# Reordering the seam between attention and the per-row blocks, and the first feed-forward tiles, of a fused transformer layer on one core

## The reference

```
x = x + attention(x)          # 32 query heads on 8 KV heads, 512 cached + 128 new keys, RMS norm, rotary, softmax
x = x + linear1(x) + low1(x)  # 512x512, and a rank-32 product chosen per row, times 0.5
x = x + linear2(x) + gated(x) # 512x512, 8 experts of rank 16; gates: top 2 of x @ Wr.T + 5*one_hot(language)
x = x + down(silu(gate(x)) * up(x))   # width 1376, each of the three with a rank-16 product chosen per row
```

## Time and profile before

| | us |
|---|---|
| median of 3 runs | 1445.12 |
| range of the 3 runs | 1442.46 to 1446.32 |
| the profiled execution, its own time | 1446.37 |
| span of the profiled execution | 1444.6 |
| PE busy (share of the span) | 1393.5 (96%) |
| DVE busy | 1100.4 (76%) |
| ACT busy | 843.5 (58%) |
| POOL busy | 808.4 (56%) |
| mean granted PE clock, share of full | 0.991 |

### The profile page before, as it was taken

One profiled execution on the slowest core, in us unless ns is written; L12 is line 12 of the kernel. 1 busy time (PEld: TensorE's weight loads), 2 busy tenths in 40 slices (PEclk: granted clock), 3 DMA queues, 4 the chain that ended last, 5 costly groups with the idle time before them and its releaser, 6 DMA issues.

```text
span 1444.6 us, 26952 instructions
## 1 busy us (share of the span) xinstructions
PE 1393.5 (96%) x8004; PEld 1210.6 (84%) x8004; DVE 1100.4 (76%) x2209; ACT 843.5 (58%) x2072; POOL 808.4 (56%) x801
## 2 busy tenths in 40 slices
PE   2899999999999999999999999999999999899999
PEld 1788888888888888888888888888888788688887
DVE  4788888888888888888888888888888566554544
ACT  1566666666666666666666667676676322433332
POOL 5555555555555666666666666666566320454342
PEclk9899999999999999999999999999999999999999
DMA  4433343333333322232322222222323440233441
GB/s 127 138 103 110 114 117 101 101 103 103 103 101 104 95 71 66 65 76 68 70 64 65 65 69 76 66 67 47 116 59 94 114 96 22 91 120 120 121 120 67
DMA packets 192705, 129.87 MB, mean 90 GB/s; under 512 B 119088, under 2 KB 159792, under 8 KB 190256
## 3 DMA queue, kind: packets, MB, share of 16 engines
q1 hardware_dynamic: 192560, 128.15, 32.1%
HBM read 125.24 MB, written 24.64 MB: 104 GB/s over the span
## 4 chain that ended last, share of the span: by engine, by line
PE 81%; SPq 12%; issue 3%; DVE 1%; DMA 1%; POOL 1%; ACT 1%; DVEq 0%
PE banks L311 19%; PE banks L312 19%; PE banks L313 19%; PE banks L1275 10%; PE banks L1252 8%; SPq L357 6%; SPq L341 3%; SPq L365 2%; PE banks L1216 2%; DMA w_raw<-in_w_att 1%; PE banks L1490 1%; PE banks L1504 1%; PE banks L1317 1%; PE banks L1443 1%; SPq L336 1%
## 5 line engine op out<-in xcount | busy, mean ns | idle before, releaser
L695 ACT ACTIVATE prob<-prob,nbias 128x640 f32<-128x640 f32 x256 | 210.4, 822 | 148.6 <-DVE nbias L908 148.6
L883 DVE TENSOR_TENSOR pt_pair<-banks,pt_pair 128x640 fp32r<-128x640 f32 x256 | 211.0, 824 | 108.3 <-ACT pt_pair L691 105.7
L908 DVE CUSTOM_DVE_ANT_0 prob<-banks,mask,q_rs 128x640 f32<-128x640 f32 x256 | 220.3, 879 | 42.8 <-PE banks L313 42.6
L1275 PE MATMUL banks<-w_pair,o_pair 128*128 128x512 f32 x768 | 224.1, 414 | 0.0
L691 ACT ACTIVATE pt_pair<-banks 128x640 fp32r<-128x640 f32 x256 | 179.3, 700 | 44.1 <-PE banks L1252 44.1
L311 PE MATMUL banks<-w_pair,x_pair 128*128 128x256 f32 (+1 forms) x512 | 179.1, 350 | 20.9 <-POOL w_pair L489 20.9
L1252 PE MATMUL banks<-ident,prob 128*128 128x128 f32 x1280 | 185.3, 276 | 3.5 <-DVE pt_pair L883 3.5
L1252 PEld LDWEIGHTS banks<-ident,prob 128*128 128x128 f32 x1280 | 147.4, 140 | 45.2 <-issue 33.2
L312 PE MATMUL banks<-w_pair,x_pair 128*128 128x256 f32 (+1 forms) x512 | 174.0, 340 | 0.0
L313 PE MATMUL banks<-w_pair,x_pair 128*128 128x256 f32 (+1 forms) x512 | 173.3, 339 | 0.0
L311 PE MATMUL banks<-kt_pair,qt_pair 128*128 128x320 f32 x512 | 164.9, 322 | 2.2 <-DVE kt_pair L883 2.2
(11 more groups left out here) (176 smaller groups left out, 3433.4 us busy)
## 6 DMA issues: line engine op xcount, KB each, us to landing
w_raw<-in_w_att SPq DMA_DIRECT2D x64, 320.0 KB, 3.2
w_raw<-in_fw SPq DMA_DIRECT2D x66, 256.0 KB, 3.3
x_raw<-in_xT SPq DMA_DIRECT2D x64, 256.0 KB, 3.2
kt_all<-in_kT SPq DMA_DIRECT2D x128, 128.0 KB, 2.5
kv_raw<-in_kv SPq DMA_DIRECT2D x416, 32.0 KB, 1.6
kt_raw<-kt_all SPq DMA_DIRECT2D x38, 256.0 KB, 3.0
kv_raw<-in_kv SPq DMA_DIRECT2D x608, 16.0 KB, 1.5
fb_all<-in_gu_b SPq DMA_DIRECT2D x32, 176.0 KB
```

The lines of the kernel that those rows point to most:

```text
L695: act.activation(prob[:, h, :], prob[:, h, :], ACT.Exp, bias=nbias[:, h:h + 1], scale=-1.0, accum_out=psum_row[:, h:h + 1]).then_inc(exped, 1)
L883: dve.tensor_tensor(pair[1], src, pair[0].bitcast(F32), ALU.subtract).then_inc(lo_sem, 1)
L908: dve.tensor_tensor_reduce(out=prob[:, h, :].rearrange("p (a n) -> p a n", a=2), in0=score_ps[h % 2][:, :, 0:HALF], in1=mask[:, n % B, :]. ...
L1275: last = pe.matmul(misc_ps, o_pair[:, j, h, :], w_pair[:, k, ds(at + h * HID, HID)], start=i == 0, stop=i == 3 * REP - 1)
```

## The change

Only the order of instructions changes; each engine has as many as before.

1. Row 0's x1 transposes on PE move from step 63 into step 62, behind the output projection's middle eight matmuls and ahead of the third probability transposes; ACT's copy and DVE's split of them move to the end of step 62. The low-rank product `lora1(0)` moves ahead of the last probability transposes of step 62 on PE, and ACT's `low_high(0)` and DVE's `lora1_low(0)` move forward in step 63.
2. In step 63 ACT does the fourth exponential ahead of the second probability copy.
3. `gu_high(0, 0)` moves from the start of stage 6 into stage 5, behind `low_high(6)`. `gu_high(1, 1)` moves from the first feed-forward step into the end of stage 6. On DVE `fb_low(0, 0)` moves to the end of stage 6 and `fb_low(1, 1)` ahead of `end_b(7)`.
4. ACT's `dn_high(0, 0)` and the sigmoid of tile 0 go ahead of the last `x3t_high`; DVE's two multiplications of tile 0 (`gated(0)`) ahead of the last `x3t_low`. Splitting `act_pair` stays in the first feed-forward step.
5. The copy and split of `db_pair` move from just before the feed-forward to behind step 4 of it.

The core of the diff:

```diff
@@ ACT, attention step
                 if n == NT - 2:
+                    x1t_high(0)
                     act.wait_ge(s_b1, 16 * 4)
@@ ACT, final_step
                 pt_high(n - 1, 3)
-                x1t_high(0)
+                low_high(0)
                 v_high(n, par)
                 exponent(n, par, 2)
                 o_high(n - 1)
                 pt_high(n, 0)
-                low_high(0)
                 to_high(ra_pair[:, 0], ra_raw[:], s_small, 16 * 6, ra_hi)
+                exponent(n, par, 3)
                 pt_high(n, 1)
-                exponent(n, par, 3)
@@ ACT, stage
                 low_high(b + 1)
+                if b == B - 3:
+                    gu_high(0, 0)
                 hgt_high(b)
                 x2t_high(b + 1)
                 if b + 2 < B:
                     x1t_high(b + 2)
+                else:
+                    gu_high(1, 1)
@@ ACT, after the stages
+            def ff_step(m, par):
+                if m > 1:
+                    gu_high(m, par)
+                    dn_high(m - 1, 1 - par)
+                    sigmoid(m - 1)
+                act_high(m - 1, 1 - par)
             for b in range(1, B - 1):
-                if b == B - 2:
-                    gu_high(0, 0)
                 stage(b)
...
             hgt_high(B - 1)
+            dn_high(0, 0)
+            sigmoid(0)
             x3t_high(B - 1)
-            act.wait_ge(s_ffs, 16 * 5 * B)
-            act.activation(db_pair[:, 0], d_b[:], ACT.Copy).then_inc(db_hi, 1)
@@ DVE, attention step, behind add_attention(n - 1)
+                if n == NT - 2:
+                    x1t_low(0)
@@ DVE, final_step
                 normalise(n, 1)
-                x1t_low(0)
                 mask_min(n, par, 2)
...
+                lora1_low(0)
                 normalise(n, 2)
                 o_low(n - 1)
                 pt_low(n, 0)
-                lora1_low(0)
@@ DVE, after the stages
+            fb_low(0, 0)
             gate_up_lora(0)
...
-            fb_low(0, 0)
+            fb_low(1, 1)
             end_b(B - 1)
+            gated(0)
             x3t_low(B - 1)
-            low(db_hi, 1, [db_pair[:, k] for k in range(2)], d_b[:], db_lo)
@@ PE, x1_transpose
+                if b == 0:
+                    pe.wait_ge(qt_lo, NT)
@@ PE, attention step
                     project_out(n - 1, 2, 10)
+                if n == NT - 2:
+                    x1_transpose(0)
                 transpose_p(n, 2)
@@ PE, final_step
                 scores(n, 1)
+                lora1(0)
                 transpose_p(n - 1, 3)
-                x1_transpose(0)
                 scores(n, 2)
                 values(n - 1, 1 - par, False)
-                lora1(0)
```

More of the change, by code:

```diff
@@ L704, in w2_high, with to_high, x1t_high @@
                 act.activation(w2_pair[:, 0, c, :], w2_raw[:, c * HID:(c + 1) * HID], ACT.Copy).then_inc(w2_hi, 1)
+            def to_high(dst, src, done, count, hi_sem, scale=1.0):
+                act.wait_ge(done, count)
+                act.activation(dst, src, ACT.Copy, scale=scale).then_inc(hi_sem, 1)
+            def x1t_high(b):
+                to_high(x1t_pair[:, 0].rearrange("p c n -> p (c n)"), x1t_ps if b else y1_ps, x1t_done, b + 1, x1t_hi)
             def step(n, par, x=True, w=True):
@@ L740, in _ @@
             steps(step)
[L742 to L747, removed]
             def x2t_high(b):
@@ L819, in gu_high, with dn_high, sigmoid, act_high @@
                 act.activation(fb_rows[par][:], fb_raw[:, par], ACT.Copy).then_inc(fb_hi, 1)
+            def dn_high(m, par):
+                act.wait_ge(s_dn[par], 16 * 2 * (m // 2 + 1))
+                if m >= 2:
+                    act.wait_ge(down_done, m - 1)
+                act.activation(fw_pair[par][:, F_DOWN:FW], fw_raw[par][:, F_DOWN:FW], ACT.Copy).then_inc(dn_hi, 1)
+            def sigmoid(m):
+                act.wait_ge(g_done, m + 1)
+                act.activation(sig[:], g_ps, ACT.Sigmoid).then_inc(sig_done, 1)
+            def act_high(m, par):
+                to_high(act_pair[par][:, 0], act_f[:], act_done, m + 1, act_hi)
+            def db_high():
+                act.wait_ge(s_ffs, 16 * 5 * B)
+                act.activation(db_pair[:, 0], d_b[:], ACT.Copy).then_inc(db_hi, 1)
+            def ff_step(m, par):
[4 more added lines that the diff above has]
+                act_high(m - 1, 1 - par)
             for b in range(1, B - 1):
-                if b == B - 2:
-                    gu_high(0, 0)
                 stage(b)
@@ L829, in _ @@
             hgt_high(B - 1)
+            dn_high(0, 0)
+            sigmoid(0)
             x3t_high(B - 1)
-            act.wait_ge(s_ffs, 16 * 5 * B)
-            act.activation(db_pair[:, 0], d_b[:], ACT.Copy).then_inc(db_hi, 1)
[L835 to L851, removed]
+            tiles(ff_step, (2, lambda: gate_up_lora_high(2)), (3, lambda: gate_up_lora_high(3)), (4, db_high),
                   (FT + 1, lambda: down_lora_high(0)))
             dn_high(2 * FT - 1, 1)
-            swish(2 * FT - 1, 1)
+            sigmoid(2 * FT - 1)
+            act_high(2 * FT - 1, 1)
             down_lora_high(1)
@@ L962, in _, with flat, x1t_low @@
             w_high(PIECES - 2, 0)
+            def flat(ap):
+                return ap.rearrange("p c n -> p (c n)")
+            def x1t_low(b):
+                low(x1t_hi, b + 1, [flat(x1t_pair[:, k]) for k in range(2)], x1t_ps if b else y1_ps, x1t_lo)
             def step(n, par, x=True, w=True):
@@ L1139, in _, with gated @@
             hgt_low(B - 1)
[L1141 to L1147 removed]
+            def gated(m):
                 dve.wait_ge(sig_done, m + 1)
@@ L1168, in add_ffn, with db_low, ff_step @@
                     dve.tensor_tensor(acc[:, b, :], ffn_bank[b % HB], acc[:, b, :], ALU.add).then_inc(ffn_added, 1)
[L1170 removed]
+            def db_low():
+                low(db_hi, 1, [db_pair[:, k] for k in range(2)], d_b[:], db_lo)
+            def ff_step(m, par):
+                if m > 1:
+                    fb_low(m, par)
+                    gated(m - 1)
+                act_low(m - 1, 1 - par)
+            fb_low(1, 1)
             end_b(B - 1)
+            gated(0)
             x3t_low(B - 1)
[L1173 to L1176 removed]
             tiles(ff_step, (2, lambda: gate_up_lora(2, used=(tg_lo, 2))), (3, lambda: gate_up_lora(3, used=(tg_lo, 3))),
[L1179 to L1180 removed]
+                  (4, db_low), (FT + 1, lambda: (down_lora(0, (tg_lo, 4)), add_ffn(0))))
+            gated(2 * FT - 1)
+            act_low(2 * FT - 1, 1)
             down_lora(1, (td_lo, 1))
@@ L1278, in project_out, with transpose4, x1_transpose @@
                     last.then_inc(wo_done, 1)
+            def transpose4(bank, src):
+                for c in range(DC):
+                    last = pe.transpose(bank[:, c * P:(c + 1) * P], src[:, c * P:(c + 1) * P], ident[:])
+                return last
+            def x1_transpose(b):
+                pe.wait_ge(added, NT - B + b + 2)
+                if b == 0:
+                    pe.wait_ge(qt_lo, NT)
+                if b == 1:
+                    pe.wait_ge(masked, REP * NT - 1)
+                transpose4(x1t_ps if b else y1_ps, acc[:, b, :]).then_inc(x1t_done, 1)
             def step(n, par, x=True, w=True):
@@ L1312, in _ @@
             steps(step)
-            def transpose4(bank, src):
-                for c in range(DC):
-                    last = pe.transpose(bank[:, c * P:(c + 1) * P], src[:, c * P:(c + 1) * P], ident[:])
-                return last
             def linear(dst, xt, w, chunks, stop):
```

24 lines of the change are left out of this document (6 added, 18 removed).

## The result

The changed kernel takes **1432.39 us** (median of 4 runs, 1431.42 to 1433.52). The kernel before, on the same chip, takes 1445.72 (median of 4, 1442.46 to 1447.65). The ratio is 0.991, with a 95% interval of 0.989 to 0.993: 13.3 us faster (about 10 to 16 by the interval), where 13.9 were forecast. The forecast time was 1431.2, the range 1427.5 to 1436.5. The profiled execution took 1431.42 us, with a span of 1429.6.

What follows compares the result with a forecast made beforehand. PE has work for 96% of the span, so reordering wins only where PE stands still. Terms 1.7 + 6.7 + 2.6 + 2.9 = 13.9 us off the 1445.12 us median gave 1431.2 us; range 1427.5 to 1436.5.

Steps and rivals of the forecast that it cites:

- Stage 6: PE's 1.52 us wait before row 7's block-1 low-rank product goes, as POOL's split no longer holds DVE's subtraction: 1.7 us.
- the 0.13 us of margin: Stage 5: DVE's instruction starts at 1194.87, POOL at 1195.0; if POOL starts first, the stall moves there, 1432.9 us, chance 0.08.
- The long pause: PE's 6.45 us pause before the second feed-forward tile's gate product vanishes with earlier splits and sigmoid: 6.7 us.
- Clock behind it: Second feed-forward tile's first 14 gate matmuls run at full clock, 2.98 us instead of 5.58: 2.6 us.
- Row 0: Steps 62 and 63: block 1 starts 1.2 us sooner, plus 1.7 if the value product keeps full clock: 2.9 us.
- the fall of the clock after the change: Rival in step 63: the clock falls anyway behind 2.2 us of pause; price 1.7 us, 1432.9 us, chance 0.22.
- Own-row product in stage 6: Tile 0's fb split delays DVE by 0.6 us, leaving 0.5 of 1.1 us room; cost 0, or 1.2 if held longer.
- The clock in step 63: If transposes do not count as activity, work between the two pauses looks thinner and the clock falls as before.
- Two short pauses set aside: Two shorter PE pauses inside attention step 63, said to stand at products whose order does not change.
- Slower after all: Rival in stage 5: ACT waits for the first tile's weights; about 1450 us, chance 0.02.

Runs made afterwards that it cites:

- tail_only: Changed kernel with row 0's move and the step-63 exponential order (item 2) taken back; 1432.47 us, ratio to the kernel before 0.9917, +1.15 us in the trace.
- values_sooner: Changed kernel with step 63's last probability copy and split moved ahead, row 0's splits and low-rank product behind them; -0.46 us in the trace.
- sigmoid_late: Changed kernel with row 7's x3 copies and splits again ahead of the down copy, tile 0's sigmoid and gating; +7.47 us in the trace.
- step_only: Changed kernel with items 3 to 5 taken back, row 0's move kept; 1441.19 us, ratio to the kernel before 0.9977, +11.18 us in the trace.
- fill_63: Changed kernel with the last chunk of row 0's first low-rank layer moved behind step 62's last output projection on PE; -0.16 us in the trace.

## Why the prediction was right

The forecast time was 1.2 us too low: 0.6 because the kernel before came out at 1445.72 and not at 1445.12, and 0.6 because the gain was 13.3 and not 13.9. The terms, in the timelines:

- **Stage 6, 1.7 us.** Measured 1.75 in the timeline, 1.79 by putting the split back. Mechanism and place confirmed, and the 0.13 us of margin came out as 0.13.
- **The long pause, 6.7 us.** Measured 6.69. But the spare time behind it came out 1 us longer than worked out. I let GpSimd hold the split of tile 1's small weights for 2.3 us, so that `gsig` would end 0.8 us ahead of PE. In the trace DVE (rows of the changed kernel) came first and GpSimd was held:

```profile
1217.20 0.68 DVE L1145 TENSOR_TENSOR fb_rows<-fb_raw,fb_rows 32x512 fp32r<-32x512 f32 x1
...
1217.22 1.81 POOL L623 TENSOR_TENSOR fw_pair<-w_raw,fw_pair 128x512 fp32r<-128x512 f32 x1
...
1219.33 0.68 DVE L1160 TENSOR_TENSOR gsig<-banks,sig 128x512 f32<-128x512 f32 x1
```

  GpSimd's split of the same size takes 1.28 us at 1108.05. `gsig` ended at 1220.0 and PE came at 1221.86: 1.8 us to spare.
- **Clock behind it, 2.6 us.** Measured 2.54.
- **Row 0, 2.9 us.** Measured 2.68. Its steps hold: pauses of 0.63 and 1.56 (about 0.7 and 1.5 forecast); the value product at 1117.62 in the old times (1117.5); block 1 at 1122.57 (1122.4 by the steps with the clock kept). What the term took for granted was the clock of the kernel before. By tail_only that kernel's order can also run with the clock kept, and then the same edit brings 1.15. So the edit's own part, the pauses, is right, and that the whole 2.9 came out is luck: the profile compared with was one in which the clock had fallen. The forecast named the fall of the clock after the change as the rival, and not its absence before it.
- **Own-row product in stage 6.** The tile-0 split was held (1.75 us instead of 0.68), 0.6 us of delay were forecast, and gating 7 ended 0.46 us ahead of PE, against 0.5. This was right.
- **Not foreseen.** GpSimd's value split holds a normalisation in step 63 in the changed kernel too (1.81 us at 1116.44). It takes 1.3 of the slack ahead of block 1, where 1.0 us are left, so it costs nothing there. It decided the fate of values_sooner.
- **The clock in step 63.** The first value matmul behind the pause of 1.56 us took 0.50 us (0.63 in the earlier trace rows) in the changed kernel, and 0.49 to 0.51 in the seven experiments that have the same two pauses. The Trainium skill, "TensorE: Matmul & The Clock Gate", Part 4, has transposes not count as activity, from which I had a fall follow as a possibility. No fall came, and no run here isolates the transposes.
- **Two short pauses set aside.** The prediction has them ahead of products; by the rows they stand ahead of transposes. They are 0.61 and 0.37 us before and after, so nothing hung on it.
- **Slower after all.** ACT's copy of tile 0 ran at 1189.88 with no idle time: the weights were there, as the rival's own row had said.

## What to carry to other kernels

Follow each pause of the bounding engine to its last releaser, and ask of that instruction not only what stands ahead of it but why it lasts so long: here the 2.3 us for a 128x8 subtraction were a collision that one move on a third engine removed. A pause of several microseconds (3.98 to 6.45 here) costs its own length and then the clock. So of two edits that each leave 4 us of it, one alone would bring some 2 us, and both bring 9.2: 6.69 + 2.54 us together, of which undoing either one lost 7.1. When executions differ by more than the effect, count from a fixed instruction of the bounding engine to the end of the span.

## What the runs showed of the hardware

**A tenth of a microsecond decides, in unchanged code too.** In stage 4 GpSimd begins six casts (3.4 us in all) as soon as a transfer lands, among DVE's small gating instructions. First the changed kernel, then sigmoid_late, whose code there is the same:

```profile
1170.24 0.17 DVE L1055 SCALAR_TENSOR_TENSOR gate<-rank,expl 128x8 f32<-128x8 f32 x1
...
1170.26 3.42 POOL L604 CAST ga_rows<-gu_a 128x512 fp32r<-128x512 f32 x6 [9.29 <-DMA d_a<-in_d_a]
```

```profile
1170.22 3.41 POOL L604 CAST ga_rows<-gu_a 128x512 fp32r<-128x512 f32 x6 [9.19 <-DMA d_a<-in_d_a]
...
1170.30 0.55 DVE L1055 SCALAR_TENSOR_TENSOR gate<-rank,expl 128x8 f32<-128x8 f32 x1
...
1172.67 0.50 PE L1381 MATMUL banks<-b_rows,low_rows 128*128 128x512 f32 x1 [0.26 <-DVE low_rows L1018]
```

DVE waits here for the end of one cast (0.57 us each), not of all six. In sigmoid_late a second small instruction, at 1171.28, takes 0.69 us where it takes 0.24 in the kernel before, and PE pauses for 0.26 us; in the changed kernel that second one alone is held (0.63 us at 1170.84), and PE doesn't pause. From the start of stage 4's first low-rank product (line 1365) to its second (line 1381) PE needs 3.61 us in the changed kernel and 4.03 in sigmoid_late. The same shows in step_only (a pause of 0.27, 4.03 us) and fill_63 (0.30, 4.06 us), and in no other profile. It makes differences of 0.4 us between two profiles meaningless without a look at this place.

**The clock is not a function of the pause.** Behind 2.07 us it fell to the lower level in the kernel before and stayed in tail_only; behind 1.56 us it stayed in all eight profiles that have this pause. Behind 3.98, 4.07 and 6.45 us (twice) it always fell. What makes the difference at 2.07 stays open: the two lists of instructions are the same there.
